# Two attention layers on one core: which queue sends the first batch's query stacks, and when batch 1's x and mask are fetched

## The reference

```python
# layer 0, x: (4, 256, 256), ctx: (4, 512, 256)
z = layer_norm(x, ln1_w, ln1_b)
q = (z @ q_w + q_b)   # 16 heads of 16
k, v = ctx @ k_w + k_b, ctx @ v_w + v_b
scores = where(mask, q @ k.T / 4, finfo.min)
h = softmax(scores) @ v @ cproj_w + cproj_b + x
h = h + gelu(layer_norm(h, ln2_w, ln2_b) @ fc_w + fc_b) @ proj_w + proj_b
# layer 1, one head
q, k, v = h @ w_q.T, ctx @ w_k.T, ctx @ w_v.T
out = h + alpha * (softmax(q @ k.T / 16) @ v) @ w_o.T
```

## Time and profile before

| | us |
|---|---|
| median of 3 timed runs | 317.65 (313.06 to 319.94) |
| profiled execution | 312.16 |
| its span | 310.4 |
| TensorE busy, share of the span | 268.6, 87% |
| DVE busy | 206.8, 67% |
| ScalarE busy | 187.8, 61% |
| GpSimd busy | 118.3, 38% |

### The profile page before, as it was taken

One profiled execution on the slowest core, in us unless ns is written; L12 is line 12 of the kernel. 1 busy time (PEld: TensorE's weight loads), 2 busy tenths in 40 slices (PEclk: granted clock), 3 DMA queues, 4 the chain that ended last, 5 costly groups with the idle time before them and its releaser, 6 DMA issues.

```text
span 310.4 us, 5591 instructions
## 1 busy us (share of the span) xinstructions
PE 268.6 (87%) x2073; PEld 195.3 (63%) x2073; DVE 206.8 (67%) x367; ACT 187.8 (61%) x351; POOL 118.3 (38%) x174
## 2 busy tenths in 40 slices
PE   3974769998788999899979997999998989898995
PEld 2670236683266676665866766665966777677974
DVE  5774777729657859576569598657388655366854
ACT  1553367759464686967454887766466678426622
POOL 3574652523111369830012688430131256324100
PEclk9997599989797999999999999999999999999999
DMA  5597552522254002124112112121130000000001
GB/s 176 173 155 104 141 157 94 163 72 67 78 154 126 12 25 67 57 74 126 64 38 99 28 59 70 34 80 51 34 130 3 0 1 2 2 0 0 2 34 36
DMA packets 21163, 21.62 MB, mean 70 GB/s; under 512 B 4608, under 2 KB 17616, under 8 KB 21136
## 3 DMA queue, kind: packets, MB, share of 16 engines
q1 hardware_dynamic: 16880, 13.09, 14.8%
q0 software_dynamic: 1648, 3.87, 4.9%
q10 hardware_dynamic: 2608, 4.30, 4.6%
HBM read 10.50 MB, written 1.05 MB: 37 GB/s over the span
## 4 chain that ended last, share of the span: by engine, by line
PE 56%; ACT 13%; POOL 11%; DVE 9%; issue 5%; DMA 3%; ACTq 2%; POOLq 0%; DVEq 0%
PE work_ps L602 10%; PE om L679 8%; PE s L652 7%; PE work_ps L589 6%; PE s L669 6%; PE work_ps L606 5%; DVE neg_max L1442 4%; ACT q_stack L1100 3%; ACT probs L1109 2%; POOL y_l L1833 2%; PE s L602 2%; DMA q_stack<-qp 2%; POOL kf L1793 1%; ACT fx L1136 1%; POOL ft L1828 1%
## 5 line engine op out<-in xcount | busy, mean ns | idle before, releaser
L1442 DVE TENSOR_REDUCE neg_max<-s 128x1 f32<-128x512 f32 x128 | 83.5, 683 | 23.1 <-PE s L652 21.9
L1109 ACT ACTIVATE probs<-s 128x512 f32<-128x512 f32 x128 | 75.3, 601 | 32.4 <-PE s L669 31.8
L652 PE MATMUL s<-k_stack,q_stack 97*128 97x512 bf16 x128 | 49.8, 424 | 8.2 <-DMA q_stack<-qp 4.9
L669 PE MATMUL s<-q_stack,k_stack 109*128 109x256 bf16 x256 | 51.8, 286 | 2.0 <-ACT probs L1109 1.0
L679 PE MATMUL om<-probs,vals 128*17 128x256 f32 x512 | 34.5, 390 | 0.2 <-ACT probs L1109 0.2
L669 PEld LDWEIGHTS s<-q_stack,k_stack 109*128 109x128 bf16 x256 | 21.0, 102 | 19.0 <-ACT probs L1109 5.0
L652 PEld LDWEIGHTS s<-k_stack,q_stack 97*128 97x128 bf16 x128 | 13.0, 102 | 28.8 <-DVE neg_max L1442 14.3
L1763 POOL CAST max_cols<-neg_max 128x8 bf16<-128x8 f32 x16 | 6.1, 381 | 63.2 <-DVE neg_max L1442 63.2
L1100 ACT ACTIVATE q_stack<-om 13x1024 bf16<-13x1024 bf16 x16 | 16.3, 1017 | 9.1 <-PE om L659 8.8
L679 PEld LDWEIGHTS om<-probs,vals 128*17 128x17 f32 x512 | 12.0, 98 | 13.7 <-issue 6.2
L1123 ACT ACTIVATE y_h<-work_ps 128x512 fp32r<-128x512 f32 x12 | 7.2, 596 | 16.3 <-PE work_ps L606 14.5
(11 more groups left out here) (328 smaller groups left out, 724.5 us busy)
## 6 DMA issues: line engine op xcount, KB each, us to landing
k_stack<-kp SPq DMA_DIRECT2D x96, 64.0 KB
q_stack<-qp SPq DMA_DIRECT2D x81, 32.0 KB
cx<-in_ctx_dram SPq DMA_DIRECT2D x4, 512.0 KB, 4.7
pcx<-in_ctx_dram ACTq DMA_DIRECT2D x3, 512.0 KB, 3.6
xz<-in_x_dram SPq DMA_DIRECT2D x4, 256.0 KB, 2.7
raw_late<-in_L_xattn_fc_w_dram POOLq DMA_DIRECT2D x1, 1024.0 KB, 5.4
raw_late<-in_L_xattn_proj_w_dram POOLq DMA_DIRECT2D x1, 1024.0 KB, 6.7
h<-in_x_dram ACTq DMA_DIRECT2D x3, 256.0 KB, 2.6
```

The source lines that it names most:

```text
L652: pe.matmul(s1[:, s1_bank(b, SLOTS * g + s), :], q_stack[0:ROW_MAX, hd, chunk(t)], k_stack[0:ROW_MAX, hd, :], start=True, stop=True).then_ ...
L669: mm = pe.matmul(s2[:, s2_bank(b, SLOTS * g + s), i * LQ:(i + 1) * LQ], k_stack[:, hd, chunk(k)], q_stack[:, hd, :], start=True, stop=True)
L1109: act.activation(probs[:, g % 2, s // 2, k:k + 2, :], s2[:, s2_bank(b, SLOTS * g + s), :].rearrange("p (k n) -> p k n", k=2), ACT.Exp).the ...
L1442: dve.tensor_reduce(neg_max[:, g % 2, s % 2, s // 2:s // 2 + 1], s1[:, s1_bank(b, SLOTS * g + s), :], AX.X, ALU.max, negate=True).then_inc ...
```

## The change

`LATE_QUERIES` becomes 1 and 3: group 1's queries go by GpSimd's queue and group 2's by SyncE's, at the place in it where group 1's stood. GpSimd sends group 1's six transfers at once when the parts are ready, where it sent group 2's and 3's together before. The mask and x of batch 1 and group 3's six transfers, which stood in front of GpSimd's key instructions, now stand behind the first split and ahead of the six weight loads. Nothing is computed differently, and each transfer moves the same bytes as before.

```diff
--- before.py
+++ after.py
@@ -127,7 +127,7 @@
 V_LN1W, V_LN1B, V_VB, V_LN2W, V_LN2B, V_FCB, VECS = 0, 2, 4, 6, 8, 10, 18
 STACK_DMAS = 2 * len(TERMS_Q) + 1
 
-LATE_QUERIES = 2, 3
+LATE_QUERIES = 1, 3
 
 
 def build(nc, x, ctx, mask, ln1_w, ln1_b, q_w, q_b, k_w, k_b, v_w, v_b, cproj_w, cproj_b, ln2_w, ln2_b,
@@ -447,7 +447,7 @@
                 late = g in LATE_QUERIES and n > 0
                 await_(eng, stacked[g], 16 * (STACK_DMAS * n - (len(TERMS_Q) if late else 0)))
                 if late and n == 1:
-                    eng.wait_ge(late_stacked[g % 2], 16 * len(TERMS_Q))
+                    eng.wait_ge(late_stacked[LATE_QUERIES.index(g)], 16 * len(TERMS_Q))
 
         def chunk(i):
             return slice(i * P, (i + 1) * P)
@@ -550,7 +550,7 @@
                 for i in [i for i, p in enumerate(TERMS_Q) if p == 0]:
                     sp.dma_start(q_stack[i * HD:(i + 1) * HD, group(0), :], qp[rows_of(0), 0, 0, :]).then_inc(stacked[0], 16)
                 stack_keys(0, 1)
-                stack_queries(0, 1)
+                stack_queries(0, 2)
                 stack_keys(0, 2)
                 stack_keys(0, 3)
 
@@ -1842,6 +1842,14 @@
                     pool.wait_ge(cx_high, b + 1)
                     pool.tensor_tensor(pc[1][:], pcx[:], pc[0][:].bitcast(F32), ALU.subtract).then_inc(cx_split, 1)
 
+            def late_queries(g):
+
+                for part, (sem_, n) in enumerate(((pre_free, pre_use(0, U_Q)), (qm_done, 1), (q_parts, 1))):
+                    pool.wait_ge(sem_, n)
+                    for i in [i for i, p in enumerate(TERMS_Q) if p == part]:
+                        pool.dma_start(q_stack[i * HD:(i + 1) * HD, group(g), :], qp[rows_of(g), part, g // 2, :])\
+                            .then_inc(late_stacked[LATE_QUERIES.index(g)], 16)
+
             def prologue():
                 pool.memset(ident[:], 0.0).then_inc(pool_step, 1)
                 pool.memset(sel_small[:], 1.0).then_inc(pool_step, 1)
@@ -1866,19 +1874,15 @@
                 pool.wait_ge(vec_done, 1)
                 pool.tensor_scalar(h[:, :, 0:P], vecs[:, V_VB:V_VB + DC].unsqueeze(2).to_broadcast([P, DC, P]), 1.0, None, ALU.mult)\
                     .then_inc(prep_step, 1)
-                pool.dma_start(mask_u[:], mask[1:2, :].partition_broadcast(P)).then_inc(next_mask_in, 16)
-                pool.wait_ge(pre_full, pre_use(0, U_ZT))
-                pool.dma_start(xz[:], x[1].rearrange("(p t) d -> p t d", t=TQ)).then_inc(next_x_in, 16)
-                for part, (sem_, n) in enumerate(((pre_free, pre_use(0, U_Q)), (qm_done, 1), (q_parts, 1))):
-                    pool.wait_ge(sem_, n)
-                    for g in LATE_QUERIES:
-                        for i in [i for i, p in enumerate(TERMS_Q) if p == part]:
-                            pool.dma_start(q_stack[i * HD:(i + 1) * HD, group(g), :], qp[rows_of(g), part, g // 2, :])\
-                                .then_inc(late_stacked[g % 2], 16)
+                late_queries(1)
                 key_rest(0, 1)
                 key_low(0, 1)
                 pool.wait_ge(dve_const, 2)
                 split_max(0, 0)
+                pool.dma_start(mask_u[:], mask[1:2, :].partition_broadcast(P)).then_inc(next_mask_in, 16)
+                pool.wait_ge(pre_full, pre_use(0, U_ZT))
+                pool.dma_start(xz[:], x[1].rearrange("(p t) d -> p t d", t=TQ)).then_inc(next_x_in, 16)
+                late_queries(3)
                 for i, w in ((2, l1_v), (3, l1_o)):
                     pool.dma_start(raw_l1[i], w.rearrange("(c p) n -> p c n", p=P)).then_inc(wo_in, 16)
                 for g in range(NG):
```

## The result

| | before | after |
|---|---|---|
| median of 4 executions, us | 315.36 (312.50 to 319.94) | 316.61 (315.44 to 316.88) |
| profiled execution, us | 312.16 | 316.82 |
| its span, us | 310.4 | 314.9 |
| mean granted clock of the span | 0.96 | 0.935 |

What follows compares the result with a forecast made beforehand. It took the chain through group 0's last q_stack transfer, slowed by GpSimd's traffic, as the bound; -2.8 + 1.1 = -1.7 us turned 312.16 into 310.5 on the profiled execution. Median forecast 315.0, range 309.5 to 319.5.

Steps and rivals of the forecast that it cites:

- The start: Group 0's last q_stack transfer, before the first max tile: with queue 0's traffic removed it lands 2.8 us sooner, bounds 0 to 3.3.
- Queue 0's share of 16.0 to 26.5 us: Sign in the prologue: GpSimd's transfer queue would take about an eighth of the DMA engines, against 42.0% before.
- Rival B: Group 0's landing follows its own transfers, not traffic: gain 0, GpSimd's issues cost +1.1 to +1.8, 313.3 to 314.0; chance 0.12.
- fixed cost of 2.0 us: Alternative estimate for group 0's last transfer: by this cost it would land at 22.7 and the sum be -2.6 us.
- GpSimd's lateness: Between the two splits GpSimd issues 8.40 us where it had 7.28, so the second split is 1.1 us late.
- Group 1's queries, x, group 3's queries: Moved transfers on GpSimd's queue: group 1's leave early enough; x and group 3's, issued after the first split, stay hidden, costing nothing.
- Rival C: x for batch 1 lands late behind the first split and DVE waits: -1.7 + 1.3 = -0.4 us, 311.8; chance 0.08.
- The sum at the second `max_rows`: Start gain and GpSimd's lateness together: -2.8 + 1.1 = -1.7 us, putting that max_rows at 40.5.
- The step that failed: Behind the second max_rows: the -1.7 us is carried unchanged to the end, 312.16 us becoming 310.5.
- rival A: Longer stop before the second max_rows lets the clock fall behind it; a 3.4 us low stretch costs 1.7: 312.2; chance 0.20.
- the argument against it: The first stop shrinks from 4.9 to 2.1 us, so the first clock fall may not come and TensorE comes warmer.

Runs made afterwards that it cites:

- experiment 5: The kernel before with 14 unread matmuls on TensorE ahead of its second max_rows: ratio 1.0015, mean 314.07 us against 314.60 without.
- experiment 1: The changed kernel, unchanged, measured again in another set of 12 executions: ratio 1.0034 to the kernel before, mean 314.96 us.
- experiment 2: The changed kernel, unchanged, measured once more in a further set of 6 executions: ratio 1.0112 to the kernel before, mean 316.60 us.
- experiment 7: The changed kernel with the mask and x of batch 1 back in their old place: ratio 0.9969, mean 313.59 us against 315.73 for the kernel before.
- experiment 3: The changed kernel with the six weight loads moved from behind the first split to slot 8, behind the second: ratio 0.9912, mean 312.93 us.
- 8 to 11: experiment 8, then three changed kernels with late weight loads and 14 matmuls before the second max_rows, the last two with further fills: ratios 0.9914, 0.9798, 0.9883.
- experiment 10: The changed kernel with late weight loads, 14 matmuls before each of two max_rows and 40 before the first max tile: ratio 0.9798, mean 308.07 us.
- experiment 4: The changed kernel with 14 unread matmuls on TensorE in the stop before the second max_rows: ratio 0.9915, mean 310.86 us.
- experiment 8: The kernel before with only the mask and x of batch 1 moved behind the first split: ratio 1.0067, mean 316.08 us against 315.57.

## Why the prediction was wrong

**The start: right in kind, a little too large.** Forecast: group 0's stack lands 2.8 us sooner, at 23.6, because the traffic of queue 0 holds it. Measured: 2.59, at 23.84. Of that 0.41 is because the transfer left earlier (20.28 for 20.69), which it also did in experiment 5, in the kernel before; the transfer itself became 2.17 shorter, and 2.10 in experiment 1 (1.36 in experiment 2). Queue 0's share of 16.0 to 26.5 us is 7.4%, where I had expected an eighth. Rival B is ruled out.

By the rule of the Trainium skill that I quoted (DMA: Bandwidth & Descriptors, section Queues, rings and completion order), an engine serves its queues in turn, so a transfer pays for what other queues have on the same engines. The three lengths of experiment 7, 5.74, 5.20 and 3.57 at 42.0%, 29.7% and 7.4%, agree. The page's fixed cost of 2.0 us, which it gives for transfers that GpSimd issues, was not reached by this one of ScalarE's: it stayed 1.6 above.

**GpSimd's lateness: right, and smaller.** Forecast 1.1, measured 0.82 (the split is 2.79 sooner at the first, 1.97 at the second). The mask's issue took 0.58 us and not 0.79, x and the queries as foreseen. GpSimd had no idle time before the second split, and experiment 3 gave the 0.8 back.

**Group 1's queries, x, group 3's queries: hidden, as foreseen.** TensorE doesn't wait for group 1's stack, and DVE takes x's statistics at 38.21 without a wait; x had landed at 37.1 (31.58 and 5.5). Rival C didn't happen in the form that I gave it. Its mechanism, the moved traffic making a later transfer late, did, with group 2's keys (8 to 11; not in the three profiles of the changed kernel itself). I had costed the keys at nothing, since they kept their place in SyncE's queue. I looked only at who issues before whom and not at what else the engines carry then.

**The sum at the second `max_rows`: right.** Forecast 40.5 (-1.7), measured 40.23 (-1.97).

**The step that failed** is the next sentence: "No engine's order changes behind it, so the shift is carried to the end". The order doesn't change, but the instructions' durations do. In the profile the stretch of low clock behind the second `max_rows` costs 2.5 us and takes the whole lead (1.8 and 3.2 in the other two). This is rival A, which I had given 0.20 and 1.7 us. It was mis-sized in two ways. The prediction took the cost of a stretch of 3.4 us, as in 81.1 to 84.5, and this one lasts 6.8; the items of the chain in it grow from 2.49 to 4.63 us. And the argument against it, that the engine comes warmer into the stop since the first one shrinks, had nothing to rest on: the first stretch of low clock, 26.4 to 40.1 before, is there after as well, at 24.5 to 38.2.

**The frame of the forecast failed too.** A gain of 1.7 us was set against a kernel whose executions lie 7 us apart, with their clock. The prediction treated that spread as noise around a fixed path. The profiled execution of before was one in which the clock held behind the second `max_rows`; whether that is its common case one profile can't tell. The difference of the means is +0.3 ± 0.5, with one fill on both sides it is -3 to -4, with two -1.5 ± 0.8 (in the filled pairs of one set the loads are late as well). That fits a gain of some two or three us which is lost where the stops are open. How much of the loss is owed to the longer stop stays open: delay alone cost +2.4 ± 0.9 for 1.5 of lateness and the fill brought 4.1 at the long stop and nothing sure at the short one, which points to the stop; experiments 3 and 7 show that falls come without it; and the mean clock over all executions, equal for both kernels, leaves room for a cause besides the clock that no run here names.

## What to carry to other kernels

Before carrying a shift of the critical path to the end, look at which clock TensorE has in the stretch that follows and at what an engine's new lateness does to its stops; where a known stop stands on the path, price the case in which the clock falls behind it, with the row lengths at both levels. A stop of 1 to 3 us that can't be shortened can be filled with a few matmuls that nothing reads: 14 of them, 1.09 us long, brought 4.1 ± 0.8 us at the lengthened stop of the changed kernel (1.85 us), nothing sure at the same place in the kernel before (1.18), and 3 to 4 at another stop of it (1.87). And before a gain of 1 or 2 us is judged, compare the means of many executions with their clocks. When transfers leave a crowded stretch, ask which transfer stands on the path in the stretch that they go to.

## What the runs showed of the hardware

The stops around which the clock fell from 2.4 to 1.2 GHz were short, 1.24 to 2.97 us; where it fell behind a stop of 1.24 or 1.85, a wait of 1.40 for `cT_l` began 1.4 us later. Dense work just before doesn't hold the clock either: in 10 it fell at 26.3, behind 40 dense matmuls and then 0.99 us of matmuls in 2.4.

It also fell while TensorE counted as busy. In experiment 10 the stretch that begins at 63.9 starts inside this row:

```profile
60.72 3.96 PE L948 MATMUL work_ps<-vecs,raw_late 128*128 128x1 f32 x32
```

These are 32 matmuls of one column each. In three other profiles (changed, 2 and 3) a stretch begins inside the same row too. So a stretch that the rows count as busy does not keep the clock up by itself; nor does this row always bring a fall: in experiment 4 it is 3.63 us long, and none followed until 79.6.

The Trainium skill (TensorE: Matmul & The Clock Gate, section What's actually happening) puts the penalty of the warm-up ramp under 1% of a typical kernel's span. That sentence is about the ramp at a kernel's start; here stretches at the lower clock recur through the run, and executions of one kernel lie 2.3% apart (311.68 to 318.91 us) along with their mean clock.

A transfer of 64 KB inside the SBUF took 9.16 us to land with the engines at 1.06 (experiment 8). One of 32 KB, the last of group 0, took 3.56 to 4.38 us in the profiles in which GpSimd's queue had 6.5 to 7.4% of the engines, and 5.69 to 6.06 where it had 40 to 43%. And a load costs its issuer: GpSimd spends 0.51 to 0.79 us on each `dma_start`, so the eight moved ones made 4.2 us of a queue that had 3.3 us of slack.
